# One fused gated cross-attention and ternary feed-forward block on one core: new orders for units, loads and engine queues, other places for two chunks, and loads paced at 3 MB under way

## The chip, the cores and the metric

The kernel runs on 1 core of one Trainium2 chip. The metric is the device time of one execution in microseconds (us), as the median of several runs.

## What is computed

```python
# x: (2, 1024, 2048) f32; ctx: (2, 2048, 2048) f32; weight: (2048, 2048) f32
def xattn(x1, x2, s1, z1, s2, z2):            # uint8 fake quantisation, scales 8/255, zero points 128
    q1 = (clip(round(x1 / s1 + z1), 0, 255) - z1) * s1
    q2 = (clip(round(x2 / s2 + z2), 0, 255) - z2) * s2
    return matmul(q1, q2)

def ffn(x, w):                                # int8 by rows, ternary weights
    s = 127 / clip(max(abs(x), -1), 1e-5)
    xq = clip(round(x * s), -128, 127) / s
    scale_w = 1 / clip(mean(abs(w)), 1e-5)
    tw = clip(round(w * scale_w), -1, 1)
    return einsum('bsi,oi->bso', xq, tw) / scale_w

x = x + tanh(g_xattn) * xattn(layernorm(x), ctx, ...)
out = x + tanh(g_ffn) * ffn(layernorm(x), weight)
```

## The kernel before

**Tiling.** Each of the 2 batches has M = 8 tiles of 128 rows (m), the first four called A, the last four Z, and C = 4 columns of 512 (c). A unit is one tile by one column, 16 matmuls of 128x128 by 512 into one PSUM bank. There are four stages of 32 units: X0 and X1 (cross-attention of batch 0 and 1), F0 and F1 (feed-forward). UNITS (L36 to L39) lists all 128 in PE's order. X0 uses all eight PSUM banks in turn, the later stages four; the other four then hold halves of a normalised tile for the row maximum (`spare`).

**The path of x.** SP loads an x tile of 1 MB in two halves into h. DVE takes bn_stats (L760), ACT the square root (L506), DVE the scale (L771 to L785, for batch 0 tile by tile, for batch 1 in groups of 4, 2 and 2). POOL quantises the tile to int8 (L389) into one of three places of tile_i8, SP issues a DMA transpose (L287, a "turn") into one of 2 places (from turn 16 on one of 4), and DVE (batch 0, A) or ACT (L530) converts it to bf16 in lhs, which has one place for each m. A place of lhs is rewritten only when the stage before has ended for this m.

**The path of ctx.** It is cut into 32 pieces of 512 KB for each batch, eight for each column. POOL (L407), at the very start ACT too (L487), quantises a piece into one of four places of ctx_i8, and ACT converts it to bf16 (L499) in a chunk, one per column. Batch 0 has four chunks: two in q2, two in the upper half of h of batch 1 (`upper`, L118), which is why x of batch 1 lands there late: the waits in load_x (L235). Batch 1 has two places, so columns 2 and 3 wait for the end of columns 0 and 1 of X1 (L498). Pieces of batch 0 land in eight stage places in the lower half of h of batch 1, pieces of batch 1 and all of the weight in a ring of four places of 512 KB.

**The path of the weight.** It is read twice, as 32 halves each time: ACT sums the magnitudes (L537), DVE and POOL make one scale of it (L859, L460), then POOL (L416) and ACT (L546) quantise the 16 weight tiles t, SP turns them and DVE (L840) or ACT (L554) makes fp8 of them. Four tiles make a ternary column c in tw, which lies over q2: columns 0 and 1 of tw wait for column 2 of X1, the others for column 3.

**The path of h.** DVE adds each finished unit to h (L851) and so frees its bank. Then follow stats_h (L796), the square root (L510), scale_h (L803 to L809), two halves by ACT (L521), two maxima by DVE (L816), peak_h (L823 to L828), all in groups of four tiles, the quantising by POOL, the turn and the conversion. SP stores finished columns (L293).

**What sets the order.** Each engine has its instructions in one queue, written out by hand, and waits on semaphores. In X0 the units go through all columns of A, then Z. In X1, F0 and F1 they go by PAIRS (L38): columns 0 and 1 of A, the same of Z, then columns 2 and 3 of A, of Z. F0 and F1 need the h tile of each m as lhs. On SP, `pace` (L226) holds a load back until at most AHEAD = 3 pieces (of 512 KB) ahead of it are under way.

```python
    PAIRS = [(m, c) for pair in ((0, 1), (2, 3)) for half in (A, Z) for c in pair for m in half]
    ...
                behind = 0
                for earlier, reached, its_size in reversed(loads):
                    if behind >= AHEAD:
                        sp.wait_ge(earlier, reached)
                        break
                    behind += its_size
```

Of the kernel before, what the change touches and what calls it, by code (L numbers as in the profile page):

```python
# [5 lines left out]
def flamingo_gated_block(nc, x, ctx, g_xattn, g_ffn, s1, z1, s2, z2, weight, out):  # L6
# [8 lines left out]
    P = 128  # L15
    B, S, D = x.shape
# [12 lines left out]
    AHEAD = 3  # L29
# [9 lines left out]
    UNITS = [(X0, m, c) for m, c in OPENING] + [(s, m, c) for s in (X1, F0, F1) for m, c in PAIRS]  # L39
# [18 lines left out]
    TURNS += [("h", 0, m) for m in A] + [("w", 0, t) for t in range(2 * TPC)]  # L58
    TURNS += [("h", 0, m) for m in Z] + [("w", 0, t) for t in range(2 * TPC, WT)] + [("h", 1, m) for m in range(M)]
# [9 lines left out]
    def by_dve(n):  # L69
        kind, b, m = TURNS[n]  # L70
        return (kind == "x" and b == 0 and m < NB) or (kind == "w" and m % 2 == 0)


    SUM_FIRST = 24
    RING = [("ctx", i) for i in range(2 * PIECES)] + [("sum", i) for i in range(SUM_FIRST)]
    RING += [("ctx", i) for i in range(2 * PIECES, C * PIECES)] + [("sum", i) for i in range(SUM_FIRST, 2 * WT)]
    RING += [("quant", i) for i in range(2 * WT)]
# [23 lines left out]
    with es:  # L101
# [16 lines left out]
        upper = h[:, 1, NB:M, :].rearrange("p m d -> p (m d)").bitcast(bf16).rearrange("p (c k n) -> p c k n", c=2, k=K)  # L118
# [24 lines left out]
        mv1, mv2 = small(M, 2), small(M, 2)  # L143
        ve, sd, rs, prod, tsd = ([small(NB) for _ in range(2)] for _ in range(5))
        hr1, mean_a = small(NB), small(NB)
# [4 lines left out]
        inv_amax = small(NB)  # L150
# [15 lines left out]
        ln1, ln2, peak = sem("ln1"), sem("ln2"), sem("peak")  # L166
# [56 lines left out]
        def _(sp):  # L223
            loads = []

            def pace(landing, value, size):  # L226
                behind = 0
                for earlier, reached, its_size in reversed(loads):
                    if behind >= AHEAD:
                        sp.wait_ge(earlier, reached)  # L230
                        break
                    behind += its_size
                loads.append((landing, value, size))

            def load_x(b, m):  # L235
                if b:
# [5 lines left out]
                    else:  # L242
                        sp.wait_ge(acc_done, units_end(X0, c=2 + (m - NB) // 2))
# [14 lines left out]
            def ring_place(i):  # L258
                if i >= NB:
                    sp.wait_ge(ring_used[i % NB], i // NB)  # L260
                pace(ring_in[i % NB], 16 * (i // NB + 1), 1)
                return ring[:, i % NB, :]

            def load_second(first, end):
                for piece in range(first, end):
                    i = RING_AT["ctx", piece]
                    c, p = piece // PIECES, piece % PIECES
                    sp.dma_start(ring_place(i).rearrange("p (k n) -> p k n", k=KP),
                                 ctx_t[1, p, :, :, c * NC:(c + 1) * NC]).then_inc(ring_in[i % NB], 16)

            def load_halves(what, first, end):
                for n in range(first, end):
                    i = RING_AT[what, n]
                    sp.dma_start(ring_place(i), w_t[n // 2][:, n % 2 * PW:(n % 2 + 1) * PW]).then_inc(ring_in[i % NB], 16)
# [20 lines left out]
            for c in range(C):  # L295
                sp.dma_start(h[:, 0, 0, c * NC:(c + 1) * NC], x_t[0][:, c * NC:(c + 1) * NC]).then_inc(x0_in[c], 16)
                loads.append((x0_in[c], 16, 0.5))
            load_x(0, 1)
            load_first(0, 1)
            load_x(0, 2)  # L300
            turn(TURN_X[0, 0])
            load_first(1, 2)
            load_x(0, 3)
            turn(TURN_X[0, 1])
            load_first(2, 4)
            turn(TURN_X[0, 2])
# [14 lines left out]
            for m in A[1:]:  # L321
                load_x(1, m)
# [663 lines left out]
```

## Time and profile before

| | us |
|---|---|
| median of 3 runs (lowest, highest) | 550.48 (550.24, 551.34) |
| the profiled execution's own time | 551.01 |
| its span, first to last instruction | 549.2 |
| PE busy, DVE busy, ACT busy, POOL busy | 466.0, 255.2, 232.6, 160.9 |
| mean granted TensorE clock | 0.95 |
| read from HBM, written | 83.89 MB, 16.78 MB |

Engines are PE (TensorE matmul), PEld (its weight load), DVE, ACT, POOL and SP; SPq is SP's own queue, which issues the DMAs. L12 is line 12 of the kernel. A releaser behind an arrow is what ended an engine's idle time. Matmuls are pipelined: the duration of one is longer than the time from one to the next, so rates are read from a run of many.

### The profile page before, as it was taken

How to read it: one execution, taken by the hardware profiler on the slowest of the kernel's cores; microseconds unless marked ns; L12 is line 12 of the kernel's file. 1: busy time of each engine (PE TensorE's matmuls, PEld its weight loads, DVE VectorE, ACT ScalarE, POOL GpSimd, SP SyncE). 2: the span in 40 equal slices, each digit the busy share in tenths (PEclk: the TensorE clock that was granted, in tenths of full speed). 3: DMA queues.
4: the chain of work that ended last, by engine and by line, in shares of the span. 5: the costliest groups of instructions: out<-in, count | busy, mean ns of one | idle time of the engine just before them, and what ended most of it. 6: DMA issues, size and time to landing. Idle time of an engine off the chain costs nothing.

```text
span 549.2 us, 5796 instructions
## 1 busy us (share of the span) xinstructions
PE 466.0 (85%) x2027; PEld 202.2 (37%) x2048; DVE 255.2 (46%) x455; ACT 232.6 (42%) x235; POOL 160.9 (29%) x122
## 2 busy tenths in 40 slices
PE   0179968989994896759899779974999999999997
PEld 0024423434441342314344334431444444444443
DVE  4732152768107963793633374937932222222221
ACT  1266645221783567847974446238631410000000
POOL 2537653213962200177211471210431100000000
PEclk9999998999996898959999889996999999999999
DMA  7969968675999888788989998982180803030322
GB/s 243 261 199 338 326 205 287 187 222 205 267 366 344 226 251 294 245 280 200 333 263 268 272 208 229 305 230 81 76 222 9 229 1 154 0 154 0 154 76 76
DMA packets 88293, 113.78 MB, mean 207 GB/s; under 512 B 54720, under 2 KB 54720, under 8 KB 88256
## 3 DMA queue, kind: packets, MB, share of 16 engines
q1 hardware_dynamic: 87392, 113.27, 68.5%
q8 instruction: 25, 0.41, 0.3%
q10 hardware_dynamic: 864, 0.00, 0.1%
q14 instruction: 12, 0.10, 0.0%
HBM read 83.89 MB, written 16.78 MB: 183 GB/s over the span
## 4 chain that ended last, share of the span: by engine, by line
PE 31%; issue 30%; POOL 15%; DMA 12%; ACT 6%; DVE 3%; SPq 3%; POOLq 0%; ACTq 0%; DVEq 0%
PE acc L725 31%; POOL ctx_i L407 10%; DMA ring<-in_L_ffn_weight 5%; POOL tile_i L389 3%; DMA turned_i<-tile_i 3%; SPq L287 2%; DMA ctx_i<-tile_i 2%; ACT acc L521 1%; POOL tile_i L416 1%; ACT q L499 1%; DMA h<-in_ctx 1%; ACT ring L537 1%; DMA h<-in_x 1%; ACT q L554 1%; ACT tile_i L546 1%
## 5 line engine op out<-in xcount | busy, mean ns | idle before, releaser
L725 PE MATMUL acc<-q,lhs 128*128 128x512 fp8e4 x1024 | 226.6, 385 | 16.6 <-DVE h L851 11.0
L671 PE MATMUL acc<-q,lhs 128*128 128x512 bf16 x753 | 182.9, 400 | 56.2 <-DVE lhs L833 25.0
L851 DVE SCALAR_TENSOR_TENSOR h<-acc,smalls,h 128x512 f32<-128x512 f32 x128 | 93.8, 748 | 152.6 <-PE acc L725 121.3
L725 PEld LDWEIGHTS acc<-q,lhs 128*128 128x128 bf16 x1024 | 101.2, 99 | 142.0 <-DVE h L851 14.8
L671 PEld LDWEIGHTS acc<-q,lhs 128*128 128x128 bf16 x768 | 75.7, 101 | 162.4 <-issue 41.6
L389 POOL TENSOR_SCALAR tile_i<-h,smalls 128x2048 int8<-128x2048 f32 x32 | 68.4, 2141 | 120.5 <-DVE smalls L785 38.1
L760 DVE BATCH_NORM_STATS2 smalls<-h 128x6 f32<-128x512 f32 x64 | 39.8, 681 | 55.7 <-DMA h<-in_x 55.6
L671 PE MATMUL acc<-h,lhs 128*128 128x512 bf16 x250 | 57.5, 387 | 6.7 <-ACT h L499 6.4
L499 ACT ACTIVATE q<-ctx_i 128x1024 bf16<-128x1024 int8 x48 | 49.6, 1052 | 26.9 <-POOL ctx_i L407 26.0
L530 ACT ACTIVATE lhs<-turned_i 128x2048 bf16<-128x2048 int8 x20 | 37.9, 1902 | 46.7 <-DMA turned_i<-tile_i 46.7
L407 POOL TENSOR_SCALAR ctx_i<-ring,smalls 128x1024 int8<-128x1024 f32 x32 | 38.1, 1195 | 51.1 <-DMA ring<-in_ctx 48.7
L816 DVE TENSOR_REDUCE smalls<-acc 128x1 f32<-128x1024 f32 x32 | 37.7, 1220 | 18.9 <-ACT acc L521 18.7
L407 POOL TENSOR_SCALAR ctx_i<-h,smalls 128x1024 int8<-128x1024 f32 x28 | 33.4, 1195 | 26.4 <-DMA h<-in_ctx 25.6
L671 PEld LDWEIGHTS acc<-h,lhs 128*128 128x128 bf16 x256 | 25.3, 100 | 38.4 <-ACT h L499 7.3
L796 DVE BATCH_NORM_STATS2 smalls<-h 128x6 f32<-128x512 f32 x64 | 39.4, 679 | 0.0
L521 ACT ACTIVATE acc<-h,smalls 128x1024 f32<-128x1024 f32 x32 | 37.3, 1194 | 4.6 <-DVE smalls L816 4.6
L416 POOL TENSOR_SCALAR tile_i<-ring,smalls 128x1024 int8<-128x1024 f32 x16 | 18.9, 1182 | 59.0 <-DMA ring<-in_L_ffn_weight 51.2
L537 ACT ACTIVATE ring<-ring 128x1024 f32<-128x1024 f32 x32 | 33.4, 1045 | 6.2 <-DMA ring<-in_L_ffn_weight 6.1
L546 ACT ACTIVATE tile_i<-ring,smalls 128x1024 int8<-128x1024 f32 x16 | 18.1, 1144 | 33.8 <-DMA ring<-in_L_ffn_weight 33.6
L506 ACT ACTIVATE smalls<-smalls 128x1 f32<-128x1 f32 (+2 forms) x11 | 2.2, 200 | 49.1 <-DVE smalls L765 49.1
L499 ACT ACTIVATE h<-ctx_i 128x1024 bf16<-128x1024 int8 x16 | 16.8, 1054 | 8.5 <-POOL ctx_i L407 8.5
L530 ACT ACTIVATE lhs<-ctx_i 128x2048 bf16<-128x2048 int8 x8 | 15.1, 1902 | 4.2 <-DMA ctx_i<-tile_i 4.2
(57 smaller groups left out, 82.8 us busy)
## 6 DMA issues: line engine op xcount, KB each, us to landing
ring<-in_L_ffn_weight SPq DMA_DIRECT2D x64, 512.0 KB, 5.6
h<-in_ctx SPq DMA_DIRECT2D x32, 512.0 KB, 6.3
ring<-in_ctx SPq DMA_DIRECT2D x32, 512.0 KB, 6.0
h<-in_x SPq DMA_DIRECT2D x30, 512.0 KB, 6.6
out<-h SPq DMA_DIRECT2D x28, 512.0 KB, 2.6
out<-h SPq DMA_DIRECT2D x8, 256.0 KB, 2.4
h<-in_x SPq DMA_DIRECT2D x4, 256.0 KB, 5.0
turned_i<-tile_i SPq DMA_TRANSPOSE x32, 4.6
```

What stands on the lines that cost most here:

```text
L389: nc.gpsimd.tensor_scalar(tile_i8[:, n % TP, :], tile, scale, offset, ALU.mult, ALU.add).then_inc(i8_ready[n % TP], 1)
L407: nc.gpsimd.tensor_scalar(ctx_i8[:, piece % NB, :], src, inv_s[:, 1:2], dz[:, 1:2], ALU.mult, ALU.add).then_inc(used, 1)
L499: nc.scalar.activation(flat(chunk(b, c)[:, p * KP:(p + 1) * KP, :]), ctx_i8[:, piece % NB, :], ACT.Copy).then_inc(ctx_ready, 1)
L521: nc.scalar.activation(spare[:, cols], h[:, b, m, cols], ACT.Identity, bias=nb2[:, t:t + 1], scale=hr2[:, t:t + 1]).then_inc(half_ln, 1)
L530: nc.scalar.activation(in_pairs(lhs[:, m, :, :]), pairs_apart(n), ACT.Copy).then_inc(lhs_act, 1)
L537: nc.scalar.activation(half, half, ACT.Abs, accum_out=w_part[:, n:n + 1]).then_inc(ring_used[i % NB], 1)
L671: done = nc.tensor.matmul(acc, lhs[:, m, k, :], chunk(b, c)[:, k, :], start=(k == 0), stop=(k == K - 1))
L725: done = nc.tensor.matmul(psum[:, bank(u), :], lhs[:, m, k, :], tw[:, c, k, :], start=(k == 0), stop=(k == K - 1))
L760: ins = V.bn_stats(s[:, 6 * c:6 * c + 6], h[:, b, m, c * NC:(c + 1) * NC])
L796: ins = V.bn_stats(s[:, 6 * c:6 * c + 6], h[:, b, m, c * NC:(c + 1) * NC])
L816: V.tensor_reduce(amax[:, t, s:s + 1], spare[:, s * PW:(s + 1) * PW], AX.X, ALU.max, apply_absolute_value=True).then_inc(half_max, 1)
L851: V.scalar_tensor_tensor(out=hc, in0=psum[:, bank(u), :], scalar=gain, in1=hc, op0=ALU.mult, op1=ALU.add).then_inc(acc_free, 1)
```

## The change

The arithmetic and its tiles stay. What changes:

- X0 runs columns 0 to 2 of A, columns 0 to 2 of Z, then column 3 of all eight tiles. X1, F0 and F1 run by whole columns: eight tiles of column 0, then column 1, and so on. The opening of X0 on PE is written out in slices of columns and pieces.
- Places: only one chunk of batch 0 lies in the upper half (column 2, over tiles 4 and 5); column 3 of batch 0 goes where column 0 was, batch 1 starts in the place of column 1, and the ternary columns are shifted by two (`ternary`). Each rewriting waits for the end of the column that lay there (`chunk_before`).
- Ring: sums of weights are put between the ctx pieces in four groups instead of two.
- LN work of batch 1 and of h is done by single tiles (x) or pairs (h), with its own semaphores for each step.
- The queues of SP, POOL, ACT and DVE are written out anew, item by item: halves and maxima are single items now, and stores of F0's columns 0 and 1 stand between the last weight loads and turns. F1's last two columns are stored by single columns for all eight tiles.
- W tiles 0 to 3 turn before tiles 4 to 7 of h of batch 0, the others after them.
- `pace` lets 6 pieces (3 MB) be under way ahead of a load, and the first four quarter loads go through it too.

```diff
-    AHEAD = 3
-    OPENING = [(m, c) for c in range(C) for m in A]
-    OPENING += [(NB, c) for c in range(C)] + [(m, c) for c in range(C) for m in Z[1:]]
-    PAIRS = [(m, c) for pair in ((0, 1), (2, 3)) for half in (A, Z) for c in pair for m in half]
+    OPENING = [(m, c) for half in (A, Z) for c in range(C - 1) for m in half] + [(m, C - 1) for m in range(M)]
+    BY_COLUMN = [(m, c) for c in range(C) for m in range(M)]
...
+    TURNS += [("h", 0, m) for m in A] + [("w", 0, t) for t in range(TPC)]
+    TURNS += [("h", 0, m) for m in Z] + [("w", 0, t) for t in range(TPC, WT)] + [("h", 1, m) for m in range(M)]
...
+        return (kind == "x" and m < NB) or (kind == "w" and m % 2 == 0)
+    RING = [("ctx", i) for i in range(PIECES)] + [("sum", n) for n in range(6)]
+    RING += [("ctx", i) for i in range(PIECES, 2 * PIECES)] + [("sum", n) for n in range(6, 20)]
+    RING += [("ctx", i) for i in range(2 * PIECES, 3 * PIECES)] + [("sum", n) for n in range(20, 2 * WT)]
+    RING += [("ctx", i) for i in range(3 * PIECES, C * PIECES)] + [("quant", n) for n in range(2 * WT)]
...
         def chunk(b, c):
-            return q2[:, c % 2, :, :] if b == 1 or c < 2 else upper[:, c - 2, :, :]
+            return q2[:, 1 - c % 2, :, :] if b else upper if c == 2 else q2[:, int(c == 1), :, :]
+        def chunk_before(b, c):
+            return {(0, 3): (X0, 0), (1, 0): (X0, 1), (1, 1): (X0, 3), (1, 2): (X1, 0), (1, 3): (X1, 1)}.get((b, c))
+        def ternary(c):
+            return tw[:, (c + 2) % C, :, :]
...
             def pace(landing, value, size):
-                behind = 0
+                behind, far = 0, 6
                 for earlier, reached, its_size in reversed(loads):
-                    if behind >= AHEAD:
+                    if behind >= far:
...
-                    else:
-                        sp.wait_ge(acc_done, units_end(X0, c=2 + (m - NB) // 2))
+                    elif m < NB + 2:
+                        sp.wait_ge(acc_done, units_end(X0, c=2))
...
+            load_x0(0, 4)
+            load_x(0, 1)
+            load_x(0, 2)
+            load_x(0, 3)
+            load_first(0, 2)
+            turn(TURN_X[0, 0])
+            load_first(2, 5)
+            load_first(8, 10)
+            turn(TURN_X[0, 1])
+            load_first(5, 6)
+            load_first(10, 12)
+            turn(TURN_X[0, 2])
+            load_first(6, 7)
+            turn(TURN_X[0, 3])
+            load_first(12, 14)
+            load_first(7, 8)
+            load_x(0, 4)
...
+            turn(TURN_X[0, 5])
+            load_first(24, 28)
             turn(TURN_X[0, 6])
+            load_first(28, 32)
+            turn(TURN_X[0, 7])
             load_x(1, 0)
...
+            load_ring(15, 21)
             turn(TURN_X[1, 4])
+            load_ring(21, 25)
             turn(TURN_X[1, 5])
             turn(TURN_X[1, 6])
+            load_ring(25, 29)
             turn(TURN_X[1, 7])
+            load_ring(29, 59)
+            turn(TURN_H[0, 0])
...
+            load_ring(89, 90)
+            store(0, 0, 0, 2)
+            load_ring(90, 91)
+            turn(TURN_W[0, 11])
...
+            store(0, 7, 0, 2)
+            turn(TURN_W[0, 15])
...
+            quant2(0, 0)
+            quant2(0, 1)
+            ctx_quant(56, 59)
+            weights_over_partitions()
+            ctx_quant(59, 62)
+            quant2(0, 2)
+            ctx_quant(62, 64)
...
+                    if chunk_before(b, c):
+                        s, sc = chunk_before(b, c)
+                        act.wait_ge(acc_done, units_end(s, c=sc))
...
+            for c in range(C):
+                for m in range(M):
+                    begin(unit(X1, m, c), TURN_X[1, m])
...
+            add(45, 49)
+            max_h(0, 1, 1)
             peak_h(0, 0)
+            add(49, 50)
             weight_sum()
...
+            add(74, 75)
             weight_fp8(10)
+            max_h(1, 2, 1)
+            add(75, 76)
```

## Rows read from the trace of the kernel before

**Rows 1.** The page, section 1: busy time of each engine.

```profile
PE 466.0 (85%) x2027; PEld 202.2 (37%) x2048; DVE 255.2 (46%) x455; ACT 232.6 (42%) x235; POOL 160.9 (29%) x122
```

**Rows 2.** Stretches: engines, clock, DMA share, GB/s.

```profile
core 0: us, PE busy (x) PEld busy (x) DVE busy (x) ACT busy (x) POOL busy (x), PEclk, DMA share, GB/s
0.00:18.20 18.20, 0.00 (x0) 0.02 (x1) 9.90 (x27) 3.88 (x5) 5.19 (x15) 1.00 0.83 241
...
96.40:153.70 57.30, 55.13 (x252) 25.01 (x256) 32.89 (x70) 20.46 (x18) 26.08 (x17) 1.00 0.80 228
153.70:302.30 148.60, 122.87 (x502) 50.69 (x511) 85.44 (x152) 100.86 (x124) 47.35 (x35) 0.90 0.91 278
302.30:377.80 75.50, 58.89 (x257) 25.77 (x258) 43.71 (x75) 36.37 (x28) 23.60 (x16) 0.91 0.87 226
```

**Rows 3.** PE timeline: start, length, instructions, idle before.

```profile
119.20 13.97 PE L671 MATMUL acc<-q,lhs 128*128 128x512 bf16 x63 [1.90 <-ACT lhs L530]
...
174.52 9.78 PE L671 MATMUL acc<-q,lhs 128*128 128x512 bf16 x31 [6.82 <-DVE h L851]
...
213.34 5.31 PE L671 MATMUL acc<-q,lhs 128*128 128x512 bf16 x16 [4.37 <-DVE h L851]
219.05 3.63 PE L671 MATMUL acc<-q,lhs 128*128 128x512 bf16 x15 [0.39 <-DVE h L851]
...
237.51 1.04 PE L671 MATMUL acc<-q,lhs 128*128 128x512 bf16 x2 [0.28 <-ACT q L499]
...
274.20 28.07 PE L671 MATMUL acc<-q,lhs 128*128 128x512 bf16 x125 [0.71 <-DVE h L851]
305.06 15.66 PE L725 MATMUL acc<-q,lhs 128*128 128x512 fp8e4 x64 [2.79 <-ACT q L554]
323.53 43.20 PE L725 MATMUL acc<-q,lhs 128*128 128x512 fp8e4 x192 [2.81 <-ACT q L554]
377.76 167.72 PE L725 MATMUL acc<-q,lhs 128*128 128x512 fp8e4 x768 [11.04 <-DVE h L851]
```

**Rows 4.** Waits of the whole span: us, times, longest.

```profile
DVE smalls L760 <- DMA h<-in_x: 55.6, 11, 16.9
```

**Rows 5.** Timeline of DVE and ACT at three gaps.

```profile
164.63 2.47 DVE L760 BATCH_NORM_STATS2 smalls<-h 128x6 f32<-128x512 f32 x4 [16.86 <-DMA h<-in_x]
...
211.52 0.18 DVE L805 RECIPROCAL smalls<-smalls 128x4 f32<-128x4 f32 x1 [10.60 <-ACT smalls L510]
...
368.09 1.29 DVE L840 TENSOR_SCALAR q<-ctx_i 128x2048 fp8e4<-128x2048 int8 x1 [6.36 <-DMA ctx_i<-tile_i]
...
371.49 1.91 ACT L554 ACTIVATE q<-ctx_i 128x2048 fp8e4<-128x2048 int8 x1 [4.91 <-DMA ctx_i<-tile_i]
...
376.97 0.74 DVE L851 SCALAR_TENSOR_TENSOR h<-acc,smalls,h 128x512 f32<-128x512 f32 x1
```

**Rows 6.** DMA: SP timeline, two stretches, landing of turns (L287).

```profile
36.67 24.84 SPq L255 DMA_DIRECT2D h<-in_ctx  x17
...
275.44 1.67 SPq L274 DMA_DIRECT2D ring<-in_L_ffn_weight  x2
...
359.63 1.25 SPq L274 DMA_DIRECT2D ring<-in_L_ffn_weight  x2
...
120.00:130.00 10.00, 9.95 (x48) 4.51 (x47) 9.77 (x18) 0.00 (x0) 0.00 (x0) 1.00 1.01 386
275.00:365.00 90.00, 84.15 (x372) 37.11 (x373) 48.76 (x81) 45.39 (x36) 26.22 (x19) 0.96 0.98 258
...
DMA to landing us min/median/max: 3.0/4.4/10.2
```

**Rows 7.** The page, section 5: costs by kind.

```profile
L499 ACT ACTIVATE q<-ctx_i 128x1024 bf16<-128x1024 int8 x48 | 49.6, 1052 | 26.9 <-POOL ctx_i L407 26.0
L530 ACT ACTIVATE lhs<-turned_i 128x2048 bf16<-128x2048 int8 x20 | 37.9, 1902 | 46.7 <-DMA turned_i<-tile_i 46.7
L407 POOL TENSOR_SCALAR ctx_i<-ring,smalls 128x1024 int8<-128x1024 f32 x32 | 38.1, 1195 | 51.1 <-DMA ring<-in_ctx 48.7
```

More of the change, by code:

```diff
@@ L233, in pace, with load_x0 @@
                 loads.append((landing, value, size))
+            def load_x0(first, end):
+                for c in range(first, end):
+                    pace(x0_in[c], 16, 0.5)
+                    sp.dma_start(h[:, 0, 0, c * NC:(c + 1) * NC], x_t[0][:, c * NC:(c + 1) * NC]).then_inc(x0_in[c], 16)
             def load_x(b, m):
@@ L256, in load_first, with load_ring @@
                                  ctx_t[0, p, :, :, c * NC:(c + 1) * NC]).then_inc(stage_in[j], 16)
[L258 to L274, printed above, removed]
+            def load_ring(first, end):
+                for i in range(first, end):
+                    if i >= NB:
+                        sp.wait_ge(ring_used[i % NB], i // NB)
+                    pace(ring_in[i % NB], 16 * (i // NB + 1), 1)
+                    what, n = RING[i]
+                    place = ring[:, i % NB, :]
+                    if what == "ctx":
+                        c, p = n // PIECES, n % PIECES
+                        sp.dma_start(place.rearrange("p (k n) -> p k n", k=KP),
+                                     ctx_t[1, p, :, :, c * NC:(c + 1) * NC]).then_inc(ring_in[i % NB], 16)
+                    else:
+                        sp.dma_start(place, w_t[n // 2][:, n % 2 * PW:(n % 2 + 1) * PW]).then_inc(ring_in[i % NB], 16)
             def turn(n):
@@ L365, in _ @@
[L365 to L380 removed]
+            load_ring(69, 70)
@@ new lines, in _ @@
+            store(0, 0, 2, 4)
+            turn(TURN_H[1, 4])
+            store(0, 1, 2, 4)
+            turn(TURN_H[1, 5])
+            store(0, 2, 2, 4)
+            turn(TURN_H[1, 6])
+            store(0, 3, 2, 4)
+            turn(TURN_H[1, 7])
+            store(0, 4, 2, 4)
+            store(0, 5, 2, 4)
+            store(0, 6, 2, 4)
+            store(0, 7, 2, 4)
+            store(1, 0, 0, 2)
+            store(1, 1, 0, 2)
+            store(1, 2, 0, 2)
+            store(1, 3, 0, 2)
@@ L857, in weight_sum @@
                 for j in range(NB):
-                    dve.wait_ge(ring_used[j], RING_AT["quant", 0] // NB)
+                    i = max(i for i, (what, n) in enumerate(RING) if what == "sum" and i % NB == j)
+                    dve.wait_ge(ring_used[j], i // NB + 1)
                 step(n_w, w_steps, V.tensor_reduce(w_sum[:, :], w_part[:, :], AX.X, ALU.add))
@@ new lines, in _ @@
+            add(6, 8)
+            stats_x(0, 6)
+            scale_x(0, 6)
+            stats_x(0, 7)
+            scale_x(0, 7)
+            add(8, 15)
+            stats_x(1, 0)
+            add(15, 18)
+            stats_x(1, 1)
+            add(18, 19)
+            scale_x(1, 0)
+            scale_x(1, 1)
+            add(19, 21)
+            stats_x(1, 2)
+            add(21, 22)
+            scale_x(1, 2)
+            add(22, 23)
+            stats_x(1, 3)
+            add(23, 24)
+            scale_x(1, 3)
```

979 lines of the change are left out of this document (597 added, 382 removed).

## The prediction

> **What bounds the kernel now.** I read the page first [rows 1]. PE is busy 85% of the span and no other engine is over 47%. Then the table by stretches [rows 2], cut where the PE timeline changes stage. After 377.76 us there is only matmul, 768 in 167.72 us [rows 3], 0.2184 us each, so 3.494 us for a unit of 16. In the stretch 96.4 to 153.7, less one gap of 1.9 us [rows 3], 256 weight loads go by in 55.4 us, so 3.46 us a unit. Four stages of 32 units at these rates are 2 x 110.7 + 2 x 111.8 = 445 us; the span is 549.2. The other 104 us lie ahead of 377.8: 18.2 before the first matmul, 24.8 in X0 (135.5 us for 110.7), 37.9 in X1 (148.6), 19.6 from there to 377.8 (75.5 us for 16 units of F0), and a tail near 3.7: the last matmul ends at 545.5. So the prize is the stretch 154 to 378, where DMA is at 0.87 to 0.91.
>
> The PE timeline [rows 3] places the gaps: 6.82 and 4.37 us in X1, seven of 0.4 to 1.7 us between 219 and 274, among them a ragged stretch at 233 to 242 where two matmuls run for each converted piece, then 2.79, 2.81 and 11.04 us. The releaser of the large ones is DVE's add (L851), and the DVE timeline [rows 5] says why: adds stood in the queue behind a bn_stats that waited 16.86 us for x (such waits are 55.6 us in all [rows 4]), then behind a scale that waited 10.60 us for ACT. The last gap has the same shape: at 368.09 DVE had waited 6.36 us for a turned weight, then for ACT's square root; the add came at 376.97. The ragged stretch is another thing: chunk c=2 of batch 1 may only be written when column 0 of X1 is done, and the order of PAIRS finishes it four units before it is wanted.
>
> **Prices.** DMA [rows 6]: 17 ctx pieces were issued in 24.84 us, 1.46 each; with the landing I take 1.50 us for a 512 KB piece of ctx. The stretch 120 to 130, at 386 GB/s, gives 1.36 for a half tile of x or weight (2.72 a tile). The stretch 275 to 365 at share 0.98 is 88.2 us of DMA for 30 half loads, 4 stores and 18 turns (counted in the SP timeline, its first and last rows are shown): (88.2 - 34 x 1.36) / 18 = 2.3 us a turn. Engines [rows 7]: quantising a piece 1.2, its conversion 1.05, an lhs conversion 1.9 on ACT; an add 0.74 [rows 5].
>
> **The change, stage by stage.** No computation is added or removed; the small LN work goes by single tiles or pairs instead of fours. That is DVE and ACT instructions of about 0.2 us (L805 in [rows 5]), some 60 more, 12 us on a DVE that is busy 46%: hidden, unless it sits ahead of an add. In X1 and later an add has 3 units (10 us) of cover, since four banks rotate.
>
> X0. Now columns 0 to 2 of A, columns 0 to 2 of Z, then column 3 of all. The A part needs 24 pieces instead of 32, but all eight x tiles are loaded among them, and piece 7 comes after pieces 8 to 13. DMA: 2 (start) + 24 x 1.50 + 8 x 2.72 + 5 turns x 2.3 + 3 (the first 18.2 us ran at share 0.83 [rows 2]) = 74.3. Quantise, convert and 8 last matmuls: 4.4, so 78.7. PE is fed piece by piece until then, as before. Then 20 units are ready with no more ctx needed for twelve of them: 69.2 us, and about 2 for x tiles 6 and 7 whose turns stand behind four pieces each. X0 ends at 150 (before 153.7). The start itself (18.2) is open: turn 0 is issued near 13 us in both kernels, now behind two more x tiles. Nothing waits for PE there, since column 0 ends with piece 7 anyhow: 0 to 4 us, the cover being the 24 pieces; I take 0.
>
> X1, by columns. All eight x tiles of batch 1 are wanted in the first column, and the lhs places come free only in X0's last column. DMA from 74.3 to the turn of tile 7: 11 turns (25.3), 24 ctx pieces (36), 13 half weights (17.7), 8 x tiles (21.8) = 101, so 175, +1.9 conversion = 177; PE wants it at 150 + 7 x 3.46 = 174. With the sums of weights that stand ahead of it on ACT I take 5 us of stall (between 0 and 16, below). After that no column waits: chunks 2 and 3 may be written from the end of columns 0 and 1, a whole column (27.7 us) ahead, and 8 pieces take about 10.6 us of POOL. That removes the ragged stretch. The x tiles 4 and 5 are freed by column 2 of X0, tiles 6 and 7 are not used as a chunk any more, so the stats of x come early, and each wait of DVE is for something some units old. On POOL the chain from unit 48 (max, peak, two quant2, three pieces, the all-reduce, three pieces, quant2, two pieces) is about 24 us long, column 3 is wanted 24.2 us later: just covered, and a slip there shows fully. X1 ends at 150 + 110.7 + 5 = 266.
>
> F0. Weights cannot turn before lhs tiles of h are converted, which now needs units 56 to 59. W0's turn goes near 249, W3's near 259, converted at 266: 1.5 us of stall, F0 starts at 267. Column 1 is due 28 us later (295): from 249, 9 half loads and 12 turns are 39.8 us and 6.3 for landing and conversion, 295. Column 2 is due at 323: 4 turns, 9 loads and one store more, 318. Column 3 is due at 351: all 22 loads, 20 turns, 8 stores are 87 us, 343 with landing. Column 3 was due at unit 84 before, now at unit 88. The stores stand ahead of weight turns on SP: each waits for the add of a unit that is done by then, its cost is its 1.36 us. I take 3 us of stall. F1 is matmul alone, as before: 111.8; T(H1,m) waits for F0 column 3, at least 24 us ahead of its use.
>
> Sum: 267.2 + 111.8 + 3 + 111.8 + 3.7 (tail) = 497.5. To this I add 5 us for short waits between three in-order queues that hand halve, max and add to each other; before, the seven gaps of 0.4 to 1.7 us in X1 came to about that [rows 3]. Span 502.5. The profiled execution was 551.01 at a span of 549.2, and the median of the three runs 550.48, so +1.3: 504 us.
>
> The pace. Before, a load waited until at most some 2 MB were under way; now 3 MB and more at the start. From ring place 4 on it binds little: the ring has four places of 512 KB. A deeper queue fills the DMA gaps at the start, and it lets turns stand behind more loads. Turns landed in 3.0, 4.4 (median) and 10.2 us [rows 6], so bounds for a turn are 3.0 and 10.2; I take 4.4 to 6, since 0.5 to 2 MB stand ahead of most.
> The Trainium skill, "DMA: Bandwidth & Descriptors", section "Queues, rings and completion order", says that on each DMA engine descriptors are consumed in ring order, loads and turns alike. By this a turn behind 3 MB would wait some 8 us at the 386 GB/s of 120 to 130 before it began; the longest landing, 10.2 us, agrees, and the median is shorter. It is the first rival.
> The same page, "Bandwidth", gives about 358 GB/s as what binds a core's HBM loads; the stretch 120 to 130 moved 386 GB/s, so the measurement decides. At 358 a half tile would be 1.46 us and tile 7 of X1 some 6 us later.
>
> **Rivals.**
> (1) Late turns. In X1 two places rotate until tile 7: at 10.2 landing + 1.9 conversion, one tile per 6.05 us instead of 3.46, six tiles: 16 us instead of 5. In F0 column 1 has no slack: + about 5. That gives 504 + 11 + 5 = 520. For: the landing of 10.2 us happened once with fewer loads ahead. Against: the first tiles are converted well before PE needs them, and the ring holds no more than 2 MB.
> (2) DMA as the only bound. If the last weight is converted as late as before (373.4, ACT at 371.49 for 1.91 [rows 5]), only the due time moves: 373.4 + 40 x 3.494 + 3.7 + 1.3 = 518. For: share 0.98 from 275 to 365. Against: share 0.91 in X1 was held by waits, and x and ctx come earlier.
> (3) Slower. One mechanism: turns, DVE's fp8 conversions and adds close a circle in F0 (a turn waits for a place that a conversion frees, which stands behind an add, whose unit waits for a weight), so that four places work as one or two. Before, 16 weights and their tiles took about 90 us for 20 turns, 4.5 each. From 249 to column 3 there are 102 us in my sum; being slower than 550 needs 46 more, 148 / 20 = 7.4 us a turn: it decides from there. With the cycle of 12.1 us over two places, 6.05 each, it ends near 504 + 19 = 523; over one place, 20 x 12.1 - 102 = 140 more, 644 us. Against: the orders put each conversion behind an add that is some units old.
> (4) It does nothing: only if every gap comes back, 550. The gaps in X1 have causes that are removed, so hardly.
>
> **Chances.** Forecast (494 to 512): 0.50. Better, 488 to 494 (no coupling loss, no stall in X1): 0.07; below 488: 0.05. Rivals 1 and 2 with their mixtures (512 to 533): 0.28. 533 to 549: 0.04. Within 0.2%: 0.01. Slower: 0.05. About 0.2% (1.1 us) is what a measurement can tell from no change. Range 488 to 533.
>
> **What would show it.** Right: matmuls of X1 start near 150 and of F0 near 267; no gap over 6 us after 80 us; in X1 no ragged stretch before column 2; DVE's wait for h<-in_x under 35 us (55.6 before [rows 4]); DMA share near 1.0 to 175 us. Wrong: L287's landing median over 7 us and PE waiting for lhs conversions in X1's first column (rival 1); the last weight load issued after 345 us (rival 2); DVE idle before L840 again with PE behind it (rival 3).

## The result and the profile after

| | before | after |
|---|---|---|
| median of 4 runs each (lowest, highest), us | 550.36 (549.05, 551.34) | 503.09 (502.18, 503.80) |
| ratio after to before, 95% interval | | 0.9142 (0.9117 to 0.9166) |
| the profiled execution, its span, us | 551.01, 549.2 | 503.80, 502.0 |
| mean granted TensorE clock | 0.95 | 0.98 |

The forecast was 504 us, in a range of 488 to 533. The change is 47 us faster. The total is right by luck: four of its terms are wrong by 5 us or more, and the errors cancel (see Point by point). The PE timeline shows the two largest. Its columns are start, length, instructions, and in brackets the idle time before and its releaser. It stands against [rows 3].

```profile
27.72 14.96 PE L836 MATMUL acc<-q,lhs 128*128 128x512 bf16 x56 [27.72 <-ACT q L604]
...
59.88 13.98 PE L836 MATMUL acc<-h,lhs 128*128 128x512 bf16 x64
73.69 27.79 PE L836 MATMUL acc<-q,lhs 128*128 128x512 bf16 x128
101.32 13.98 PE L836 MATMUL acc<-h,lhs 128*128 128x512 bf16 x64
115.13 38.15 PE L836 MATMUL acc<-q,lhs 128*128 128x512 bf16 x176
154.44 7.07 PE L836 MATMUL acc<-q,lhs 128*128 128x512 bf16 x32 [1.15 <-DVE lhs L1039]
163.34 7.07 PE L836 MATMUL acc<-q,lhs 128*128 128x512 bf16 x32 [1.84 <-ACT lhs L634]
171.11 58.87 PE L836 MATMUL acc<-q,lhs 128*128 128x512 bf16 x272 [0.70 <-ACT lhs L634]
233.95 2.25 PE L836 MATMUL acc<-q,lhs 128*128 128x512 bf16 x6 [3.98 <-DVE h L1057]
242.17 1.04 PE L836 MATMUL acc<-q,lhs 128*128 128x512 bf16 x2 [5.97 <-ACT q L604]
244.25 1.98 PE L836 MATMUL acc<-q,lhs 128*128 128x512 bf16 x4 [1.04 <-ACT q L604]
248.41 26.80 PE L836 MATMUL acc<-q,lhs 128*128 128x512 bf16 x116 [2.17 <-ACT q L604]
276.95 221.29 PE L942 MATMUL acc<-q,lhs 128*128 128x512 fp8e4 x1024 [1.74 <-ACT q L656]
```

How to read it: X0's twelve units of A end at 73.7. From there X0's other 320 matmuls follow without a gap, 0.216 us each, so X0 ends at 142.7, and the run of 176 already holds 48 of X1. X1 has two groups of gaps: 3.7 us in its first column (1.15 + 1.84 + 0.70), and 13.2 us at the head of its last column, from unit 56 on (3.98 + 5.97 + 1.04 + 2.17). It ends at 275.2. F0 and F1 are a single run of 1024 matmuls, 0.2161 us each.

The stages, with [rows 3] for before: X0's end came 11.0 us earlier (153.7 to 142.7); X1 took 132.5 us where it had taken 148.6, 16.1 less; from there to the end of F0's sixteenth unit it is 57.1 us (276.95 + 256 x 0.2161 = 332.3) where it had been 75.5, 18.4 less; the last 768 matmuls took 166.0 against 167.7. Together 47.2 us, which is the difference of the spans.

A gap is not all that a stall costs. Of the 16.1 us that X1 gained, 8.9 are idle time of PE (25.7 us before, 16.9 after) and 7.2 are its busy time for the same 512 matmuls (122.87 us in [rows 2], 115.64 below), at a granted clock of 0.90 before and 0.94 after.

The stretches, to be laid beside [rows 2]: us, busy time of each engine, granted clock, DMA share, GB/s.

```profile
0.00:80.00 80.00, 51.04 (x222) 21.92 (x223) 49.13 (x110) 41.12 (x44) 47.73 (x44) 1.00 1.03 331
...
80.00:142.70 62.70, 62.70 (x292) 28.43 (x291) 47.85 (x98) 25.61 (x36) 31.02 (x21) 1.00 1.03 332
142.70:275.20 132.50, 115.64 (x514) 49.85 (x511) 92.14 (x161) 92.60 (x111) 50.65 (x36) 0.94 0.86 250
```

Until X0 ends, the DMA share is 1.03. The kernel before showed this for its first 80 us:

```profile
0.00:80.00 80.00, 49.39 (x204) 20.15 (x208) 34.76 (x76) 36.84 (x39) 42.14 (x42) 1.00 0.85 264
```

So 26.5 MB had moved by 80 us instead of 21.1. DVE's wait for x of batch 1, 55.6 us in [rows 4], is now

```profile
DVE smalls L978 <- DMA h<-in_x: 15.9, 8, 5.4
```

**The gap that no term of the sum had.** These are POOL's timeline around unit 56, and what the trace has for the line of the all-reduce, L501 (durations in ns, first and last start in us). "issue" means that the engine waited for nothing that the profile shows:

```profile
222.13 1.20 POOL L471 TENSOR_SCALAR ctx_i<-ring,smalls 128x1024 int8<-128x1024 f32 x1 [1.32 <-DMA ring<-in_ctx]
232.07 0.40 POOL L501 PARTITION_ALL_REDUCE smalls<-smalls  x1 [8.74 <-issue]
239.84 3.56 POOL L471 TENSOR_SCALAR ctx_i<-ring,smalls 128x1024 int8<-128x1024 f32 x3 [7.37 <-issue]
...
L501 POOLq MODIFY_POOL_CONFIG  x2: 11/11/11, 223.3 to 223.3; - x2
```

The all-reduce shows 0.40 us, but POOL did nothing else from 223.33 to 239.84: 16.5 us for one instruction. Ahead of it the sequencer of POOL ran two MODIFY_POOL_CONFIG at 223.3, and the all-reduce started 8.74 us later. What fills the 7.37 us behind it has no row. The DVE timeline has the other half:

```profile
222.12 1.22 DVE L1022 TENSOR_REDUCE smalls<-acc 128x1 f32<-128x1024 f32 x1
232.51 0.15 DVE L1070 TENSOR_SCALAR smalls<-smalls 128x1 f32<-128x1 f32 x1 [9.17 <-POOL smalls L501]
...
233.15 0.75 DVE L1057 SCALAR_TENSOR_TENSOR h<-acc,smalls,h 128x512 f32<-128x512 f32 x1
```

DVE waited 9.17 us for the sum, with an add queued behind: PE's gap of 3.98 us ends on that add. Pieces 59 to 62 of ctx stood behind the all-reduce on POOL: the gaps of 5.97, 1.04 and 2.17 us end on the conversions of 59, 60 and 62.

In the kernel before, the same instruction (L460) cost nothing that can be measured (experiment 1), and these rows of its POOL timeline and of its line suggest why:

```profile
277.21 0.40 POOL L460 PARTITION_ALL_REDUCE smalls<-smalls  x1 [13.00 <-DVE smalls L859]
285.18 2.21 POOL L416 TENSOR_SCALAR tile_i<-ring,smalls 128x1024 int8<-128x1024 f32 x2 [7.56 <-issue]
...
L460 POOLq MODIFY_POOL_CONFIG  x2: 11/11/11, 264.2 to 264.2; - x2
```

The two configuring instructions ran at 264.2, 13 us ahead, while POOL waited for DVE anyhow, and behind the all-reduce stood only weight tiles for F0. The new order has it with five of column 3's eight pieces still to come.

The Trainium skill, "GPSIMD Engine Reference", section "Instruction dispatch", says that the first call to a freshly loaded kernel of POOL pays a load of about 6 us that no instruction shows. The 8.74 us here and 7.07 us below agree in kind and are longer; of the 7 us behind the instruction it says nothing. Whether a second call would cost less is not shown: each kernel here has only one.

### The profile page after: what moved, and what is told of

The parts are those of the page before. It is cut to its first block, busy times and chain, and to the rows that moved or that the text cites. A ratio compares the mean times of both kernels' runs of the same rounds, so it can differ in the third digit from the quotient of the medians.

```text
span 502.0 us, 5951 instructions
## 1 busy us (share of the span) xinstructions
PE 450.7 (90%) x2048; PEld 200.3 (40%) x2048; DVE 290.8 (58%) x523; ACT 226.3 (45%) x241; POOL 165.9 (33%) x121
## 4 chain that ended last, share of the span: by engine, by line
PE 62%; issue 16%; DMA 7%; POOL 6%; ACT 5%; SPq 2%; DVE 1%; POOLq 0%; ACTq 0%; DVEq 0%
PE acc L942 44%; PE acc L836 18%; POOL ctx_i L471 5%; DMA h<-in_ctx 3%; ACT q L604 2%; DMA ctx_i<-tile_i 2%; POOL tile_i L453 1%; DMA ring<-in_L_ffn_weight 1%; DMA h<-in_x 1%; SPq L286 1%; ACT acc L625 1%; ACT lhs L634 0%; ACT q L656 0%; DVE smalls L992 0%; ACT L610 0%
## 5 line engine op out<-in xcount | busy, mean ns | idle before, releaser
L836 PE MATMUL acc<-q,lhs 128*128 128x512 bf16 x896 | 202.1, 387 | 45.8 <-ACT q L604 38.1
L942 PE MATMUL acc<-q,lhs 128*128 128x512 fp8e4 x1024 | 221.3, 379 | 1.7 <-ACT q L656 1.7
L836 PEld LDWEIGHTS acc<-q,lhs 128*128 128x128 bf16 x896 | 87.7, 99 | 159.4 <-ACT q L604 44.1
L942 PEld LDWEIGHTS acc<-q,lhs 128*128 128x128 bf16 x1024 | 100.1, 98 | 123.0 <-DVE h L1057 2.2
L453 POOL TENSOR_SCALAR tile_i<-h,smalls 128x2048 int8<-128x2048 f32 x32 | 70.6, 2211 | 76.6 <-DVE smalls L992 29.7
L604 ACT ACTIVATE q<-ctx_i 128x1024 bf16<-128x1024 int8 x56 | 57.0, 1049 | 53.2 <-POOL ctx_i L471 42.8
L978 DVE BATCH_NORM_STATS2 smalls<-h 128x6 f32<-128x512 f32 x64 | 39.8, 680 | 16.0 <-DMA h<-in_x 15.9
L1022 DVE TENSOR_REDUCE smalls<-acc 128x1 f32<-128x1024 f32 x32 | 38.6, 1220 | 16.8 <-ACT acc L625 16.6
L634 ACT ACTIVATE lhs<-turned_i 128x2048 bf16<-128x2048 int8 x16 | 30.3, 1903 | 37.3 <-PE acc L942 25.1
L641 ACT ACTIVATE ring<-ring 128x1024 f32<-128x1024 f32 x32 | 33.7, 1054 | 11.6 <-DMA ring<-in_L_ffn_weight 10.7
L836 PE MATMUL acc<-h,lhs 128*128 128x512 bf16 x128 | 28.0, 379 | 0.0
L836 PEld LDWEIGHTS acc<-h,lhs 128*128 128x128 bf16 x128 | 12.5, 98 | 15.1
L1039 DVE CAST lhs<-turned_i 128x2048 bf16<-128x2048 int8 x8 | 10.7, 1339 | 5.5 <-DMA turned_i<-tile_i 5.4
L604 ACT ACTIVATE h<-ctx_i 128x1024 bf16<-128x1024 int8 x8 | 8.4, 1054 | 5.6 <-POOL ctx_i L471 5.3
```

Source lines behind the costliest of these rows:

```text
L453: nc.gpsimd.tensor_scalar(tile_i8[:, n % TP, :], tile, scale, offset, ALU.mult, ALU.add).then_inc(i8_ready[n % TP], 1)
L604: nc.scalar.activation(flat(chunk(b, c)[:, p * KP:(p + 1) * KP, :]), ctx_i8[:, piece % NB, :], ACT.Copy).then_inc(ctx_ready, 1)
L634: nc.scalar.activation(in_pairs(lhs[:, m, :, :]), pairs_apart(n), ACT.Copy).then_inc(lhs_act, 1)
L641: nc.scalar.activation(half, half, ACT.Abs, accum_out=w_part[:, n:n + 1]).then_inc(ring_used[i % NB], 1)
L836: done = nc.tensor.matmul(acc, lhs[:, m, k, :], chunk(b, c)[:, k, :], start=(k == 0), stop=(k == K - 1))
L942: done = nc.tensor.matmul(psum[:, bank(u), :], lhs[:, m, k, :], ternary(c)[:, k, :], start=(k == 0), stop=(k == K - 1))
```

## The experiments

Each was timed against the kernel before on the same chip, so ratios are what is compared; "after" is 0.9142.

### 1. The all-reduce taken away, in both kernels

After:

```diff
-                nc.gpsimd.partition_all_reduce(w_all[:, :], w_sum[:, :], P, bass.bass_isa.ReduceOp.add).then_inc(w_all_done, 1)
+                nc.gpsimd.tensor_copy(w_all[:, :], w_sum[:, :]).then_inc(w_all_done, 1)
```

> The changed kernel with the sum over partitions on POOL replaced by a copy: the scale of the weights is then that of each partition's own sum, so that part of the computation is left out. In the changed kernel POOL stood idle 8.74 us before and 7.37 us after this instruction of 0.40 us, and PE then lost 13.2 us at the head of column 3 of X1. If that is the cause, those gaps go and the time is 488 to 492 us; if the gap is from the ring or from ACT, it stays at 500 or more.

Measured: 490.72 us, ratio 0.8904 (0.8854 to 0.8954). The end of its PE timeline:

```profile
170.39 61.02 PE L836 MATMUL acc<-q,lhs 128*128 128x512 bf16 x282 [0.69 <-ACT lhs L634]
231.78 0.60 PE L836 MATMUL acc<-q,lhs 128*128 128x512 bf16 x2 [0.37 <-ACT q L604]
234.99 0.60 PE L836 MATMUL acc<-q,lhs 128*128 128x512 bf16 x2 [2.60 <-ACT q L604]
236.16 26.47 PE L836 MATMUL acc<-q,lhs 128*128 128x512 bf16 x114 [0.57 <-ACT q L604]
263.97 221.17 PE L942 MATMUL acc<-q,lhs 128*128 128x512 fp8e4 x1024 [1.33 <-ACT q L656]
```

The gaps at unit 56 fall from 13.2 to 3.5 us and F0 starts 13.0 us earlier. So 9.6 of the 13.0 us are idle time. Another 2.3 us are PE's busy time for the same 400 matmuls (90.9 to 88.7 us): in the kernel after, the matmuls between the gaps ran at a granted clock of 0.50, which is 1.2 GHz, and a pair of them took 1.04 us where it takes 0.60 here. The last 1.1 us are small differences in X1's first column and at F0's head. The 3.5 us that are left have another cause: POOL waited for the ring between these pieces, once for 2.55 us.

Before, the same edit at L460:

> The kernel before with the sum over partitions on POOL replaced by a copy: that part of the computation is left out. There the all-reduce stands behind all ctx pieces; POOL's 13.0 us before it are covered by the wait for the sums, and only the 7.6 us behind it delay weight tile 1. By my theory it costs little there: 546 to 550. If it costs as in the changed kernel (12 us), 538.

Measured: 547.81 us, ratio 0.9979 (0.9949 to 1.0009). In one place the instruction costs nothing that can be measured, in the other 13 us. POOL's timeline of this run shows the cover in the old place: with a mere copy there, POOL waits as long for DVE, and then for a weight half:

```profile
279.72 0.19 POOL L460 COPY smalls<-smalls 128x1 f32<-128x1 f32 x1 [13.22 <-DVE smalls L859]
283.78 2.25 POOL L416 TENSOR_SCALAR tile_i<-ring,smalls 128x1024 int8<-128x1024 f32 x2 [3.87 <-DMA ring<-in_L_ffn_weight]
```

So it is the place in POOL's queue that decides what the instruction costs.

### 2. The all-reduce moved behind the last ctx piece

```diff
             ctx_quant(56, 59)
-            weights_over_partitions()
             ctx_quant(59, 62)
             quant2(0, 2)
             ctx_quant(62, 64)
+            weights_over_partitions()
...
-            weight_scale()
             add(52, 53)
...
             add(55, 57)
+            weight_scale()
```

> The changed kernel with the all-reduce moved on POOL from between pieces 58 and 59 to behind piece 63, and DVE's weight_scale moved behind add(55, 57). If the 16 us that it takes of POOL are free at that place, 490 to 494 us; but the h tiles 2 and 3 and the first weight tiles stand behind it, so by my theory it wins only in part: 493 to 500. If its place doesn't matter, 503.

Measured: 501.91 us, ratio 0.9112 (0.9073 to 0.9151): 1.2 us below after (1.7 by the ratios), less than the 3 to 10 expected, and the two intervals overlap. Its PE and POOL timelines:

```profile
234.15 0.39 PE L836 MATMUL acc<-q,lhs 128*128 128x512 bf16 x1 [2.11 <-ACT q L604]
235.32 26.09 PE L836 MATMUL acc<-q,lhs 128*128 128x512 bf16 x112 [0.79 <-ACT q L604]
271.32 223.26 PE L942 MATMUL acc<-q,lhs 128*128 128x512 fp8e4 x1024 [9.90 <-ACT q L656]
...
241.25 0.40 POOL L501 PARTITION_ALL_REDUCE smalls<-smalls  x1 [7.07 <-issue]
248.51 2.04 POOL L453 TENSOR_SCALAR tile_i<-h,smalls 128x2048 int8<-128x2048 f32 x1 [6.86 <-issue]
```

Column 3's gap is 2.9 us, and a gap of 9.90 us stands at F0's head instead. POOL is again held for 14.3 us, and now the tiles of h and of the weight are behind it. Neither of the two places tried in the new queue is free of work that is needed soon.

### 3. The sum over partitions on PE

A ones column, made once at the start by POOL, is broadcast as weights, and one f32 matmul sums the partial sums of all partitions into PSUM. POOL has no all-reduce at all.

```diff
+                step(n, G.memset(w_all[:, :], 1.0))
...
-            weights_over_partitions()
...
+                    if unit(X1, m, c) == 50:
+                        pe.wait_ge(w_steps, 1)
+                        pe.wait_ge(acc_free, 49)
+                        nc.tensor.matmul(psum[:, 0, 0:1], w_all[:, :].to_broadcast([P, P]), w_sum[:, :], start=True, stop=True).then_inc(w_all_done, 1)
...
-                step(n_w, w_steps, V.tensor_scalar(w_mean[:, :], w_all[:, :], 1.0 / (D * D), EPS, ALU.mult, ALU.max))
+                step(n_w, w_steps, V.tensor_scalar(w_mean[:, :], psum[:, 0, 0:1], 1.0 / (D * D), EPS, ALU.mult, ALU.max))
...
             add(50, 51)
+            weight_scale()
```

> The changed kernel, complete, with the sum over partitions made by one f32 matmul of a column of ones (broadcast to 128) against the partial sums, into a PSUM bank between units 50 and 51, in place of the all-reduce on POOL. If POOL's all-reduce holds up the pieces of column 3, this is as fast as leaving the reduce out (490.7 us): 489 to 493. If the wait of PE for the partial sums (ready at 216.7, unit 50 ends near 222) costs, up to 3 us more. A time over 498 would speak against the cause.

Measured: 491.24 us, ratio 0.8916 (0.8886 to 0.8946). PE waits in front of it for the partial sums, since ACT has only just summed the last weight half:

```profile
218.25 0.59 PE L938 MATMUL acc<-smalls 128*128 128x1 f32 x2 [5.58 <-DVE smalls L1072]
218.70 46.56 PE L836 MATMUL acc<-q,lhs 128*128 128x512 bf16 x204
265.10 221.18 PE L948 MATMUL acc<-q,lhs 128*128 128x512 fp8e4 x1024
```

The gap at unit 56 is gone, and 5.58 us of wait for the partial sums came in by the choice of place, more than the 3 us allowed for. So the same edit two units later, with the bank of another unit (`psum[:, 2, 0:1]`) and `weight_scale()` behind `add(52, 53)`:

> The changed kernel, complete, with the sum over partitions by one f32 matmul as in a5, but between units 52 and 53, since in a5 PE stood 5.58 us for the partial sums between units 50 and 51. If that wait was all of the loss left in X1 by the sum, 484 to 488 us (a5: 491.2). If the scale of the weights now comes too late for the first weight tiles, the gap goes to the head of F0 and the time stays near 491.

Measured: 488.67 us (486.95 to 490.35), ratio 0.891 (0.8879 to 0.8941); 0.7 us above what was expected.

```profile
219.22 0.28 PE L938 MATMUL acc<-smalls 128*128 128x1 f32 x2
219.36 3.61 PE L836 MATMUL acc<-q,lhs 128*128 128x512 bf16 x15
223.60 10.10 PE L836 MATMUL acc<-q,lhs 128*128 128x512 bf16 x45 [0.62 <-DVE smalls L1076]
233.88 24.82 PE L836 MATMUL acc<-q,lhs 128*128 128x512 bf16 x112 [0.18 <-ACT q L604]
260.70 222.86 PE L948 MATMUL acc<-q,lhs 128*128 128x512 fp8e4 x1024 [1.99 <-ACT q L656]
```

The matmul waits for nothing and takes 0.28 us (0.59 behind the wait above); the 0.62 us further on are PE's wait until DVE has read the bank. F0 starts at 260.7, 16 us earlier than after. This is the fastest version of this study, some 60 us below before. The two ratios differ by less than their intervals: that the later place beats the earlier is seen only in the one profiled execution of each, where F0 starts 4.4 us earlier and the span is 2.7 us shorter.

### 4. The pace

The change lets 6 pieces be under way; here 3 and 12 (in `pace`, `behind, far = 0, 3` and `0, 12`), and 6 in the kernel before (`AHEAD = 6`).

> The changed kernel with only the pace set back from 6 to 3 pieces. If the deeper queue matters only at the start, as I now hold, X0 ends later than the 142.7 us of the changed kernel, and all after it shifts: 505 to 509 us instead of 503, and X1 on is the same, since the ring has four places. Rival: turns behind more loads cost more than the filled gaps give: 500 or less. Rival: the pace is the larger part of the gain: over 515.

> The changed kernel with pace 12, in fact no limit but the places. If places bind already, 502 to 504 us. If late turns are the danger (rival 1 of the prediction), turns of x land later than the median 5.4 us of the changed kernel, over 7, and the time is 506 or more.

> The kernel before with only the pace of 6. My theory: the orders hold it, so 547 to 551 us (550.4). If the pace alone were the gain, under 530.

| far | kernel | us | ratio (95%) | DMA share, 0 to 80 us | landing of turns, median, us |
|---|---|---|---|---|---|
| 3 | after | 503.94 | 0.9145 (0.9089 to 0.9201) | 1.02 | 5.6 |
| 6 | after | 503.09 | 0.9142 (0.9117 to 0.9166) | 1.03 | 5.4 |
| 12 | after | 502.90 | 0.9117 (0.9050 to 0.9185) | 1.03 | 6.2 |
| 3 | before | 550.36 | 1 | 0.85 | 4.4 |
| 6 | before | 546.64 | 0.9911 (0.9876 to 0.9945) | 0.88 | 4.2 |

In the new orders the depth makes no difference that can be measured; the expectation for 3 (505 to 509) missed, and X0 ended only 0.6 us later there. In the old ones it is worth 0.9%, 5 us, a little more than expected (547 to 551): there a gap of 5.66 us at 78 to 84 us became 1.85. With 3 pieces the new queues reach a DMA share of 1.02 where the old ones have 0.85, so it is the new order and not the depth that keeps DMA full. Which part of the order does it (x tiles among the ctx pieces, or the opening) was not taken apart.

### 5. Late places for x

Tiles 6 and 7 of batch 1 are loaded when X0 has ended, as if a chunk still lay there.

```diff
                         sp.wait_ge(acc_done, units_end(X0, c=2))
+                    else:
+                        sp.wait_ge(acc_done, units_end(X0, c=3))
...
-            load_x(1, 6)
-            load_x(1, 7)
...
             turn(TURN_X[1, 3])
+            load_x(1, 6)
+            load_x(1, 7)
```

> The changed kernel with the x tiles 6 and 7 of batch 1 loaded as late as the old places forced it: after X0 has ended, ahead of ring load 15. If free places for early x are a part of the gain in X1, DVE's statistics of tile 6 hold adds and the later turns back, and X1's first column loses some 10 us: 509 to 518. If DMA had slack there and the order of columns is all, 503 to 505.

Measured: 516.25 us, ratio 0.9369 (0.9327 to 0.9411).

```profile
156.69 5.93 PE L838 MATMUL acc<-q,lhs 128*128 128x512 bf16 x16 [6.84 <-DVE lhs L1041]
166.54 16.49 PE L838 MATMUL acc<-q,lhs 128*128 128x512 bf16 x62 [3.93 <-DVE lhs L1041]
...
DVE smalls L980 <- DMA h<-in_x: 28.1, 10, 11.3
```

DVE's waits for x go from 15.9 to 28.1 us and F0 starts 12.7 us later (289.67). So two early tiles are worth 13 us, more than a quarter of the change.

### 6. Chunks written late

The prediction's reason for the ragged stretch of before was that a chunk could only be written four units before its use. Here chunks 2 and 3 of batch 1 get just that lead in the new kernel:

```diff
-                        act.wait_ge(acc_done, units_end(s, c=sc))
+                        act.wait_ge(acc_done, units_end(s, c=sc) + (4 if s == X1 else 0))
```

> The changed kernel with one more condition: chunks of columns 2 and 3 of batch 1 may be written only four units before they are wanted, as with PAIRS, instead of eight. Four units are 13.8 us, eight pieces take 10.6 us of POOL but ACT has halves and sums between them; I expect stalls at the head of columns 2 and 3, 8 to 15 us in all: 511 to 518. If the lead of eight units is not needed, 503 to 505.

Measured: 502.57 us, ratio 0.9124 (0.9085 to 0.9163), the same as after, with no new gap. The expectation (511 to 518) missed clearly. The condition did bind for column 2, where ACT now waits for PE:

```profile
188.58 2.00 ACT L604 ACTIVATE q<-ctx_i 128x1024 bf16<-128x1024 int8 x2 [7.35 <-PE acc L836]
```

There a lead of four units is enough. For column 3 it did not bind: ACT comes to its first piece at 218.65 in the kernel after and at 219.68 here, when column 1 and four units more have long ended (216).

### 7. The sums of weights moved, in the kernel before

In the ring of before, 24 sum halves stand ahead of the ctx pieces of column 2. Here eight of them go behind:

```diff
-    SUM_FIRST = 24
+    SUM_FIRST = 16
...
-            weight_sum(16, 18)
             for m in A:
                 halve(0, m)
-                if m < 3:
-                    weight_sum(18 + 2 * m, 20 + 2 * m)
...
+            weight_sum(16, 24)
```

> The kernel before with eight of the 24 sums of weight halves that stood in the ring ahead of column 2's ctx pieces moved behind all ctx pieces (ring, SP and ACT). If the ring's order made the ragged stretch at 233 to 242, and not the end of column 0, it goes, but DVE waits for the later sums: 542 to 549. If it is the lead of four units, the stretch stays: 550 or more.

Measured: 555.49 us, ratio 1.0112 (1.0044 to 1.0179), where 542 to 549 was expected: slower, but by less than 2%.

```profile
215.08 29.16 PE L669 MATMUL acc<-q,lhs 128*128 128x512 bf16 x125 [7.83 <-DVE h L849]
244.77 0.59 PE L669 MATMUL acc<-q,lhs 128*128 128x512 bf16 x2 [0.53 <-ACT q L499]
...
250.73 0.61 PE L669 MATMUL acc<-q,lhs 128*128 128x512 bf16 x2 [2.60 <-ACT q L499]
...
268.91 12.31 PE L669 MATMUL acc<-q,lhs 128*128 128x512 bf16 x47 [10.39 <-DVE h L849]
```

The ragged stretch at 233 to 242 [rows 3] is gone: one run of 125 matmuls goes through it. But column 3's pieces are ragged now, and at 268.91 PE waits 10.39 us for an add that stands behind maxima, whose halves ACT makes only after the sums. So the first half of the reason is shown (the pieces were late because sums stood ahead of them in the ring; in the kernel before POOL waited 38.3 us at one stretch for them), while the lead of four units was as before. The late sums took back more than that gain. The new kernel has the sums in three groups, of 6, 14 and 12 halves (the list of changes says four); that this is what spares it both losses is argued, no run puts them back.

### 8. More DMA in F0

To tell slack from a DMA bound, 16 extra stores of 512 KB go among the last weight loads, 16 x 1.36 = 22 us of DMA:

```diff
+                if b == 0 and c0 == 0:
+                    for other in (0, 2):
+                        there = slice(other * NC, (other + 2) * NC)
+                        sp.dma_start(out_t[M + m][:, there], h[:, 0, m, cols]).then_inc(stored[m % NB], 16)
```

> The changed kernel with 16 more stores of 512 KB, two behind each of the eight stores of batch 0's columns 0 and 1, into rows of the output that are written over later; 16 x 1.36 = 22 us more of DMA among the last weight loads and turns. If DMA bounds F0 (rival 2), the time grows by all of it, 525 us. If weights have slack, as column 3's (converted at 343.2, wanted at 359.9 in the changed kernel), it grows by 22 - 16.7 = 5 or less: 503 to 510.

Measured: 510.13 us, ratio 0.9294 (0.9259 to 0.9330).

```profile
304.96 48.51 PE L948 MATMUL acc<-q,lhs 128*128 128x512 fp8e4 x224 [0.55 <-ACT q L662]
357.94 8.77 PE L948 MATMUL acc<-q,lhs 128*128 128x512 fp8e4 x32 [4.47 <-DVE h L1063]
368.60 138.29 PE L948 MATMUL acc<-q,lhs 128*128 128x512 fp8e4 x640 [1.89 <-ACT q L662]
```

Of 22 us of DMA, 6.9 show as gaps, and 7.0 in the time. In the kernel after, the last weight tile was converted at 343.2 and due at 276.95 + 24 x 3.46 = 360.0, 16.8 us of slack, which leaves 5 of the 22. So DMA does not bound F0, and slack near that size is there. The largest gap, 4.47 us, stands two units ahead of column 3 and ends on an add: DVE had waited 5.25 us for a turned weight with that add behind. Column 3 itself then waits 1.89 us. The gap of 0.55 us at 304.96 stands at column 1, where slack was nothing.

The gain at F0 (18.4 us) was not taken apart: no run has F0 alone in the old order of units. That whole columns bring it is argued from the timelines, not shown.

## Point by point

**X0.** Forecast 150, measured 142.7. The DMA sum was too high: the last of the 24 pieces was converted at 69.92, where 74.3 + 1.2 + 1.05 says 76.5. DMA moved 364 GB/s from 20 to 60 us beside its turns. Then A's last 64 matmuls ran unbroken, so PE and no longer DMA ended A at 73.7 (forecast 78.7), and the 2 us for x tiles 6 and 7 did not come. The 69.2 us for the rest are right (69.0). The first matmul at 27.7 instead of 18.2 cost nothing, as the sum took it: PE then had 56 in a row.

**X1.** Forecast 115.7 us, measured 132.5. In the first column 5 us of stall were forecast, 3.7 came, with the releaser that was named. The ragged stretch before column 2 is gone, but the reason given was wrong: not the moment when a chunk may be written (experiment 6), but sums ahead of its pieces (experiment 7). The step that failed is the chain on POOL from unit 48 on: "about 24 us long, column 3 is wanted 24.2 us later: just covered, and a slip there shows fully". The prediction gives the all-reduce no time of its own in that chain: in the trace of after, POOL's other items of it are 15.7 us, behind 7.1 us from the end of unit 48 to the first quant2, so about 1 us was left for it. It takes 14 to 16.5 us of POOL's queue. The slip showed as 13.2 us of gaps, of which 3.5 stay without the all-reduce (experiment 1). The trace of before already held a part of the price, as 7.56 us of "issue" behind L460 and as the configuring instructions at 264.2; the prediction does not read them. The gaps are 11.9 us over the 5 forecast. The rest of the miss, 4.9 us, is PE's busy time: the 12 matmuls between the gaps took 5.27 us where 2.6 is the usual rate, and the 116 behind them 26.80 us, 0.231 each, 1.7 over it. The granted clock was 0.50 from 236 to 250 us.

**F0 and F1.** Forecast 226.6 us with 3 us of stall, measured 221.3 with none. Half of that is the stall, the other half the rate: 0.2161 us a matmul where [rows 3] gave 0.2184, 2.3 us over 1024. The due times held closely: for column 1 the sum had 295 against 295, no slack, and W7 was converted at 304.4 when it was wanted at 304.6. Column 3 was to have 8 us and had 16.8. The tail was 3.8 for 3.7.

**The 5 us for short waits** between queues appeared nowhere. It was taken from a misread timeline: between 219 and 274 us the kernel before has thirteen gaps of PE, not seven, from 0.28 to 2.16 us, 11.7 us together. The terms against the forecast, for the span: X0 -7.3, X1 +16.8, F0's head +0.2, F0 and F1 -5.3, tail +0.1, coupling -5: together -0.5 us (502.5 forecast, 502.0 measured). That the total came out is luck. With the all-reduce at no cost, as the sum had it, the forecast would have been 13 us too high (490.7 in experiment 1).

**Two slips of the sum** change nothing: quantising, converting and 8 last matmuls are 1.2 + 1.05 + 1.7 = 4.0, not 4.4, and at 358 GB/s the 45 half tiles up to tile 7 of X1 would cost some 5 us more, not 6.

**The rivals.** (1) Late turns: they landed in 3.0, 5.4 (median) and 10.7 us, a median 1 us above [rows 6], and X1's first column lost 3.7 us, not 16. (2) DMA as the only bound: false by experiment 8; the last weight load was issued at 327.6, before it at 359.6 [rows 6]. (3) The circle in F0: no gap. The sign named for it, DVE waiting with PE behind, did come once, in X1, for another reason. (4) No change: false, the time fell by 47 us.

**The signs.** X1 began at 142.7 (150 was named), and DVE's wait for x fell to 15.9 us (under 35). F0 began at 277 and not near 267, which told of the gap at unit 56, where the ring stood still (DMA share 0.00 from 232.5 to 239.8). The DMA share was to be near 1.0 to 175 us: it was 1.03 to 142.7, but 0.88 from there to 175, long before that gap; why is open. The largest gap after 80 us is 5.97, just under the 6 that was named, so that sign alone would have called this stage good.

## What to carry to other kernels

POOL's all-reduce costs its queue 14 to 16.5 us, not the 0.40 us that its row shows: in a trace read the idle time marked "issue" on both sides of such an instruction, and count it for everything behind it before you move it between work that is needed soon. A sum over partitions of one column is a matmul with ones, 0.28 us, if the partial sums are ready. Order the loads so that each is possible when its turn comes; the depth of the queue was then of no account here. And in a forecast price a gap of PE above its length, by the busy time that the same matmuls took in a stretch with gaps.

## What was not expected of the hardware

- The all-reduce of a 128x1 tile shows 0.40 us in all three kernels that were looked at, with POOL idle 8.74 and 7.37 us around it in one, 7.07 and 6.86 in the second, and 7.56 us behind it in the kernel before. With the first part it is a MODIFY_POOL_CONFIG that comes before; what the second is stays open.
- An f32 matmul of 128x128 by 1 is two instructions, 0.28 us together.
- A gap costs PE more than itself. In F0 and F1 the granted clock was 1.00, the level of 2.4 GHz, and a matmul took 0.2161 us. PE stood still from 229.97 to 233.95 and again for most of the time to 248.41. The granted clock was 0.62 from 234 to 236, 0.50 from 236 to 250, the level of 1.2 GHz, and 1.00 again from 252. The 116 matmuls from 248.41 on took 0.231 us each, the first of them at the low level. In experiment 1, with gaps of only 3.5 us in all, the clock fell too, to 0.57 from 236 to 240, and the last 114 matmuls took 0.232 each.
